# Issuing part of a small-transfer batch from ScalarE's queue in a fused condition-and-attention kernel

## The reference, cut to what matters

```
x = x + einsum('bct,bcd->bdt', x, w0[conditions])          # 32 batches
q, k, v = x Wq^T, x Wk^T, x Wv^T                           # 16 heads of 64
s = (beta q) k^T / sqrt(64), causal                        # beta = min(cond, 4)
out = x + (softmax(s) v) Wo^T
```

## Time and profile before

| | |
|---|---|
| median of 3 runs | 1571.63 us |
| span of the profiled execution (first to last instruction) | 1569.4 us |
| outside the span, against the median | 2.2 us |
| PE busy | 1559.1 us, 99% of the span |
| PE's weight loads, beside it | 1311.9 us, 84% |
| DVE, ACT, POOL busy | 980.4, 818.9, 856.6 us (62, 52, 55%) |
| transfers | 341.46 MB, 65.8% of 16 engines' time on SP's queue, 1.4% on ACT's |

### The profile page before, as it was taken

The page is one execution under the profiler, slowest core; times in us unless marked ns, Lnnn a source line. Parts: engine busy times, 40 slices in busy tenths (PEclk is TensorE's granted clock), DMA queues, the critical chain, the costliest instruction groups (busy, mean ns, idle before and its releaser), DMA issues.

```text
span 1569.4 us, 23424 instructions
## 1 busy us (share of the span) xinstructions
PE 1559.1 (99%) x7563; PEld 1311.9 (84%) x7563; DVE 980.4 (62%) x1748; ACT 818.9 (52%) x2221; POOL 856.6 (55%) x752
## 2 busy tenths in 40 slices
PE   9999999999999999999999999999999999999999
PEld 7888888888888888888888888888888878888887
DVE  6844454443367777777766777777777754555553
ACT  6645545543366666666666666666666522222220
POOL 1545645643255566557555566675577544555552
PEclk9999999999999999999999999999999999999999
DMA  9958888865856766667677466666675696444442
GB/s 329 334 212 275 307 285 297 301 214 215 308 182 197 206 207 199 210 188 199 186 240 238 152 172 212 186 182 201 182 195 159 222 367 238 168 161 167 163 163 85
DMA packets 192299, 341.46 MB, mean 218 GB/s; under 512 B 23986, under 2 KB 116402, under 8 KB 185010
## 3 DMA queue, kind: packets, MB, share of 16 engines
q1 hardware_dynamic: 191026, 331.59, 65.8%
q10 hardware_dynamic: 1152, 8.39, 1.4%
HBM read 184.70 MB, written 134.22 MB: 203 GB/s over the span
## 4 chain that ended last, share of the span: by engine, by line
PE 98%; DMA 1%; SPq 1%; POOL 0%; issue 0%; DVE 0%; ACT 0%; DVEq 0%
PE p_PJ L710 22%; PE p_PJ L711 22%; PE p_PJ L712 22%; PE p_SC L712 6%; PE p_SC L711 6%; PE p_SC L710 6%; PE p_PV L815 4%; PE p_LP L710 1%; PE p_PV L710 1%; PE p_PV L712 1%; PE p_PV L711 1%; PE p_LP L711 1%; PE p_LP L712 1%; PE p_PV L841 1%; PE p_LP L841 1%; DMA out<-t_xr 1%
## 5 line engine op out<-in xcount | busy, mean ns | idle before, releaser
L711 PE MATMUL p_PJ<-t_XL,t_WH 128*128 128x512 f32 x1008 | 394.1, 391 | 0.0
L710 PE MATMUL p_PJ<-t_XH,t_WH 128*128 128x512 f32 x1008 | 394.1, 391 | 0.0
L712 PE MATMUL p_PJ<-t_XH,t_WL 128*128 128x512 f32 x1008 | 392.1, 389 | 0.0
L1035 ACT ACTIVATE t_PP<-t_PP,t_st 128x128 f32<-128x128 f32 x512 | 199.5, 391 | 175.4 <-DVE t_st L1211 173.9
L1333 POOL TENSOR_TENSOR t_PP<-t_PP,t_st 128x512 f32<-128x512 f32 x128 | 133.4, 1042 | 205.7 <-DVE t_st L1215 205.7
L712 PEld LDWEIGHTS p_PJ<-t_XH,t_WL 128*128 128x128 f32 x1008 | 189.3, 188 | 40.4
L710 PEld LDWEIGHTS p_PJ<-t_XH,t_WH 128*128 128x128 f32 x1008 | 190.0, 188 | 33.8
L711 PEld LDWEIGHTS p_PJ<-t_XL,t_WH 128*128 128x128 f32 x1008 | 190.0, 188 | 32.3
L1229 DVE TENSOR_REDUCE t_AT<-p_PV 64x256 f32<-64x512 f32 x252 | 171.2, 679 | 23.7 <-ACT t_AC L1053 12.0
L1339 POOL TENSOR_TENSOR t_AT<-t_AT,t_AC 128x256 f32<-128x256 f32 x126 | 117.2, 930 | 125.5 <-DVE t_AT L1229 125.5
L1336 POOL TENSOR_TENSOR t_PS<-t_PT,t_PS 128x512 fp32r<-128x512 f32 x122 | 157.7, 1293 | 0.0
(11 more groups left out here) (254 smaller groups left out, 3545.8 us busy)
## 6 DMA issues: line engine op xcount, KB each, us to landing
t_XH<-xth_scratch SPq DMA_DIRECT2D x56, 512.0 KB, 6.5
t_XL<-xtl_scratch SPq DMA_DIRECT2D x56, 512.0 KB, 6.9
t_PT<-t_TB SPq DMA_DIRECT2D x580, 32.0 KB, 2.3
v_scratch<-t_VR SPq DMA_DIRECT2D x64, 256.0 KB, 4.5
xth_scratch<-t_XH SPq DMA_DIRECT2D x16, 1024.0 KB, 4.0
xtl_scratch<-t_XL SPq DMA_DIRECT2D x16, 1024.0 KB, 6.5
t_VX<-v_scratch SPq DMA_DIRECT2D x32, 512.0 KB, 5.7
at_scratch<-t_AT SPq DMA_DIRECT2D x126, 128.0 KB, 3.5
```

The costliest lines, as they stand in the source:

```text
L710: pe.matmul(bank, lh, rh, start=first, stop=False, skip_group_check=goes_on)
L711: pe.matmul(bank, lh, rl, start=False, stop=False, skip_group_check=goes_on)
L712: return pe.matmul(bank, ll, rh, start=False, stop=last, skip_group_check=goes_on)
L1035: act.activation(PP[:, u, h, :], PP[:, u, h, :], ACT.Exp, bias=st[:, 0, u, h:h + 1], scale=1.0, accum_out=st[:, 1, u, h:h + 1]).then_inc(a ...
```

## The change

Of the ten transfers of a cell, the four with i = 3 are issued by ACT on its own queue, in a new function `act_move_p`, with the same waits as SP's and with a semaphore of their own, `l_Pd`. SP issues the other six. In ACT's program the new function stands in the loop over ticks between the exponentials and the loads of Wo and `PS` copies that are due at the same tick; its place is the tick of `move_at`, as SP's. Each reader of `l_P` now waits for 96 for a cell there and for 64 on `l_Pd`.

```diff
-        act_pt, pool_pt, l_P = sem("pt_high"), sem("pt_low"), sem("load_pt")
+        act_pt, pool_pt, l_P, l_Pd = sem("pt_high"), sem("pt_low"), sem("load_pt"), sem("load_pt_last_rows")
...
+        def act_move_p(n):
+
+            act.wait_ge(dve_t, 2 * n + 2)
+            if n == 0:
+                act.wait_ge(pool_z, 5)
+            elif n >= 2:
+                act.wait_ge(pool_pt, 2 * n - 2)
+            if n == 59:
+                act.wait_ge(pool_z, 6)
+            for j in range(4):
+                src = turned(n)[96:128, j].rearrange("a u q -> a (u q)")
+                act.dma_start(p_tile(n)[32 * j:32 * j + 32, 3, :], src).then_inc(l_Pd, 16)
...
+                for n in move_at(tick):
+                    act_move_p(n)
                 for k, low in O_fetch(tick):
                     if k >= 4:
                         act_load_wo(k, low)
                 for P in half_at(tick):
                     n = P // 2
-                    act.wait_ge(l_P, 160 * (n + 1))
+                    act.wait_ge(l_P, 96 * (n + 1))
+                    act.wait_ge(l_Pd, 64 * (n + 1))
...
             elif k == 0:
-                dve.wait_ge(l_P, 160 * n)
+                dve.wait_ge(l_P, 96 * n)
+                dve.wait_ge(l_Pd, 64 * n)
...
-                            pool.wait_ge(l_P, 160 * 64)
+                            pool.wait_ge(l_P, 96 * 64)
+                            pool.wait_ge(l_Pd, 64 * 64)
...
-            for i in range(4):
+            for i in range(3):
                 for j in range(i + 1):
                     src = turned(n)[32 * i:32 * i + 32, j].rearrange("a u q -> a (u q)")
                     sp.dma_start(p_tile(n)[32 * j:32 * j + 32, i, :], src).then_inc(l_P, 16)
```

## The result

The changed kernel takes 1619.09 us (median of 4 runs, 1618.22 to 1620.32) beside 1571.72 for the kernel before (median of 4): 47.4 us more, a ratio of 1.0304 (95% interval 1.0291 to 1.0317). The forecast was 1597 in a range of 1569 to 1630, slower. The direction and the loop hold; the size was 25 us and is 47.

The account below looks back on a forecast made before the run. PE was taken to bound the kernel, with the change closing a loop from one cell's transposes to the next: 1571.6 us plus 28.8 for 60 cells, less 4 in the last cell, gave 1597 us, range 1569 to 1630.

Parts of the forecast that it names:

- the loop: ACT's wait and four issues delay `KH` and, through DVE, the next cell's transposes: 13.82 us a cell against 13.34.
- PE has no room and SP's issuing does not hold it: PE is busy 1559.1 of 1569.4 us; SP's issuing holds it up nowhere but perhaps at the end (3.7 us).
- From the wait to KH: On ACT, from the transposes' end through four issues (2.45 us) to the start of `KH`: 2.53 us.
- I don't add to it: Issues made on ACT's and SP's queues at once cost about what each costs alone: 0 added to ACT's 2.45 us.
- moderate contention: Rival: issues on two queues slow one another, ACT's four take 2.7 to 2.9 us; about 1616 us, chance 0.15.
- From KH to the mask: On DVE, from `KH`'s start through `KL` and the even half's reductions to the masks: 3.50 us.
- From the mask to the transposes: Masks, maxima, exponentials, Q's copy and subtraction, normalization and two transposes: 7.79 us, with no idle time to absorb a delay.
- The sum: In each cell 2.53 + 3.50 + 7.79 = 13.82 us against 13.34: 0.48 lost, times 60 is 28.8 us.
- The last cell: SP's six issues shorten the path to PE's 3.7 us wait for `PS` by 2.5 us; gain taken as 4 us.
- The clock's part: After PE's final stall, about 5.6 us at half clock lose 2.8 us, saved if the shorter stall keeps the clock.
- No loop: Rival: ACT's four issues cost under 1.97 us together, leaving only the gain at the end; about 1567 us, chance 0.15.
- Turns: Rival: ACT's four issues alternate with four of SP's, 5.0 us together; about 1750 us, chance 0.06.

## Why the prediction was right or wrong

- **PE has no room and SP's issuing does not hold it: right.** With SP's issues cut to six and the loop opened (ACT's behind `KH`), the time is 1571.47: SP's gain is worth nothing.
- **From the wait to KH: right in kind, short by 0.07 us, and by 0.33 with a collision.** I took 2.53 from transposes to `KH`; it is 2.60 (641.47 to 644.07), because a copy starts 0.11 after the last issue, not 0.05. SP's price held on ACT: an issue takes 0.614 in the median where SP's takes 0.591, and four take 2.46 where I had 2.45.
- **"I don't add to it": the step that failed.** I judged the overlap from pairs of loads that had not begun in the same instant, and added nothing for contention. Here the release by one semaphore makes the second issues coincide every time, and 0.26 us falls on ACT in 45 cells. That is 12 us. It is what I had called moderate contention, at 0.27 in place of 0.25 to 0.45 us a cell and in two thirds of the cells. The range held because it took in this rival; the forecast's own band, 1577 to 1610, did not reach 1619.
- **From KH to the mask, 3.50: measured 3.51.** The even half's reductions and not the scores release the masks, as forecast. **From the mask to the transposes, 7.79: measured 7.79.** The run with `QL` moved shows that this part counts in full.
- **The sum.** A cell without a collision takes 13.90 where I had 13.82, and 0.56 more than before, not 0.48. 62 x 0.56 is 35; with 12 for collisions it is 46 to 47, and 47.5 was measured. My 28.8 lacks 6 for the gaps and the two steps I left out, and 12 for the collisions. I also put 2.2 us outside the span; the executions of the changed kernel have 1.3 to 1.4 there (1618.38 against a span of 1617.0).
- **The last cell, -4 us: wrong.** The step that failed is "this chain is 4 x 0.627 = 2.5 us shorter": with six issues in the last cell alone DVE went on 1.0 us later, not 2.5 sooner, as the landing of the store of `AT` grew from 2.1 to 5.3 us. I took the chain's length as issuing; it is landing, behind megabytes of loads. The 7.90 us that an earlier store took to land stood in the same rows, and I did not ask what made it so long. The stall became 4.2 us, not 1 or 2. The clock's part was smaller than I had it: the chip granted half the clock for 3.4 us after the stall, where it was 6.8 before, so PE is busy for 303.0 us in place of 304.0 after the last transposes, and that is the 0.4 us gained there with a stall 0.5 us longer.
- **The rivals.** No loop: excluded, though the point where it would start was right: three issues take 1.82 us and cost nothing, with a collision 2.08 and 0.17 a cell. Turns, the rule of exclusive use in the Trainium skill (Perfetto Trace Analysis, section Per-engine timelines): four issues beside six would have taken 5.0 us and took 2.46 or 2.72, so most of an issue's profiled time is not exclusive. The 0.26 us of one issue is a sign of something shared. Single issues of 1.5 to 1.65 us, on ACT with five issues a cell and with SP's later, may be another, but the kernel before has such issues on SP too, up to 1.63, with nothing on ACT's queue beside them.

## What to carry to other kernels

An issue costs its engine nothing while dispatched work remains to be run, and its full 0.6 us where the engine is drained; so ask of a moved issue not how idle the engine is but what stands behind it and who waits for that. A wait and a few issues can close a loop from one iteration to the next; then add up the loop against the iteration's length, since every 0.1 us beyond it is paid in each iteration. And a chain of issues ahead of a late transfer is the cause only if the transfer lands quickly: look first at whether the DMA engines are full.

## What the runs showed of the hardware that I had not expected

- Two queues released by the same semaphore run their first issues side by side with 0.01 us lost, and in the second one of them takes 0.82 to 0.88 us instead of 0.6. Who loses is stable over long stretches (in the trace of the changed kernel SP in the cells from 461 to 669 us but for one, ACT from 683 on but for one and the last). ACT loses from the same cell on, the twentieth, and not in the same later one, with three issues, with five and with `QL` moved (a few single cells aside), so it goes with the place in the program and not with chance; the reason is left open. Shifted by 1.1 us, the fourth issue takes 0.72 instead.
- ACT's queue issues transfers while the instructions dispatched before them still run, and before all of them have started: in the run with the issues behind `KH`, the first two issues take from 646.64 to 647.93, and the second `KH` copy starts at 647.19.
- A store issued earlier into full DMA engines landed later: 847.6 to 852.8 us after the transposes of cell 0 in the run with the last cell alone, 849.7 to 851.8 us before.
